# Gate and up of a routed feed-forward with the weights held in the array, and shared tiles without products of their own

## The chip, the cores and the metric

One core of a Trainium2 chip (trn2) runs the kernel. The time is device microseconds of one execution; three executions of the kernel before gave 442.81, 445.03 and 445.61 us.

## The reference

A transformer block in f32 over 1024 tokens of 256 values: attention with 16 heads, mixed with a linear attention, and behind it a feed-forward of 8 experts of which each token takes two.

```python
def _L0_ffn_ref(x, router_w, gate_w, up_w, down_w):
    B, S, H, F, E, K = (2, 128, 256, 688, 8, 2)
    b, s, h = x.shape
    xf = x.reshape(-1, h)
    logits = xf @ router_w.T
    top_v, top_i = jax.lax.top_k(logits, K)
    probs = jax.nn.softmax(top_v.astype(jnp.float32), axis=-1).astype(logits.dtype)
    combine = jnp.sum(jax.nn.one_hot(top_i, E, dtype=x.dtype) * probs[..., None], axis=1)
    g = jnp.einsum('th,efh->etf', xf, gate_w)
    u = jnp.einsum('th,efh->etf', xf, up_w)
    y = jnp.einsum('etf,ehf->eth', jax.nn.silu(g) * u, down_w)
    out = jnp.einsum('te,eth->th', combine, y)
    return out.reshape(b, s, h)
x = x + _L0_attn_ref(_layernorm(x, axis=-1), ...)
x = x + _L0_ffn_ref(_layernorm(x, axis=-1), ...)
```

## The kernel before, in words

The kernel is written for the five engines one by one, each with its own order of work and semaphores between them. The first 280 us are attention; the feed-forward's weights are fetched meanwhile (GpSimd, `load_gate_up`, one transfer for an expert), and the routing of the first half of the tokens is done in between. The expert part follows.

**Rows and tiles.** Each token's normalised row of 256 values, with its weight, its number and whether the expert is its first or second choice, is scattered by GpSimd into a list for its expert in memory (`scatter`, `xg_d`). The lists are worked off in tiles of 128 rows (`TILES`): tile A of an expert is rows 0 to 127 of its list, B rows 128 to 255, and a shared tile M takes rows 256 to 287 of four experts, 32 of each. The order is A of experts 0 to 4, M of experts 0 to 3 and of 4 to 7, B of experts 0 to 7, A of experts 5 to 7: 18 tiles. Rows beyond 288 of an expert would go through a loop behind it (`more`), which is skipped when there are none.

**One tile.** SyncE loads the rows (`load_xg`). TensorE turns them (`turn_x`, line 1480), VectorE copies them out of PSUM (`xgT_copy`, lines 1111 and 1107) and notes weights and token numbers (`take_meta`). TensorE multiplies with the turned rows held in the array and the expert's gate and up weights streamed, 4 chunks of 344 columns with two halves of H each (`columns`, `gate_up`; all matmuls pass the helper on line 1227). Gate is in PSUM banks 0 and 1, up in 2 and 3. ScalarE applies SiLU (line 792) and VectorE multiplies it with up (`hidden`, line 1115). The product has its 688 values along the free dimension; TensorE turns it in six blocks (`turn_hidden`, line 1491), VectorE copies it (`hidT_copy`, lines 1123 and 1124), and TensorE multiplies it with the down weights, six chunks of 256 columns (`down`, `products`). For a shared tile each of these calls is made four times, for strips of 32 rows. ScalarE weights the result (`tile_weigh`, line 796), and GpSimd adds its rows into memory with an indirect transfer (`add_y`, line 647): once for a tile, twice for a shared one (tokens of first and of second choice apart).

**The order.** From tile 3 on TensorE runs `gate_up(t)`, `turn_x(t + 1)`, `down(t - 1)`, `turn_hidden(t)`; the first three tiles are threaded by hand between the end of attention and the routing of the second half of the tokens (`post(1, ...)`). VectorE runs `take_meta(t)`, `xgT_copy(t + 1)`, `hidden(t)`, `hidT_copy(t)`. An addition waits for the landing of the one before it. The sum of the first 15 tiles (`DIRECT`) is made in `sum_d`; when these have landed, SyncE copies it to the output (line 504), and the last three tiles are added there. These are the lines in which GpSimd's order is set:

```python
if t:
    pool.wait_ge(y_added, 16 * adds(t - 1))
if t == DIRECT:
    pool.wait_ge(out_done, 16)
pool.wait_ge(y_ready, t + 1)
for k in range(K if shared(t) else 1):
    if k:
        pool.wait_ge(y_added, 16 * adds(t) - 16)
    add_rows(t, k, sum_d if t < DIRECT else out_v, y_added)
```

Of the kernel before, what the change touches and what calls it, by code (L numbers as in the profile page):

```python
# [14 lines left out]
P = 128  # L15
# [5 lines left out]
FB = [P, P, P, P, 88, 88]  # L21
FO = [sum(FB[:i]) for i in range(len(FB))]
FN = F // 2
# [3 lines left out]
UR = 32  # L27
# [53 lines left out]
def block_kernel(nc, x_d, w_d, rope_d, const_d, gate_d, router_d, gu_d, dn_d, out_d):  # L81
    ctx = ExitStack()
    with ctx:
# [50 lines left out]
        yt = words(A + 12288, NY + 1, H)  # L134
        tmp_odd = words(A + 14336, 4, HALF)
# [78 lines left out]
        xgT = keep(2, HB, P)  # L214
        act_g = keep(2, F)
        hid = keep(2, F)
        hidT = keep(2, len(FB), P)
# [8 lines left out]
        def sem(name):  # L226
# [34 lines left out]
        more_in, more_x_ps, more_x, more_gu, more_silu, more_hid, more_h_ps, more_h, more_y, more_yt, more_taken, more_added, more_done = (  # L261
            sem(n) for n in ("more_in", "more_x_ps", "more_x", "more_gu", "more_silu", "more_hid", "more_h_ps", "more_h",
# [7 lines left out]
        hidT_ps, hidT_ready, y_ps, y_ready, y_added = (sem(n) for n in  # L270
            ("hidT_ps", "hidT_ready", "y_ps", "y_ready", "y_added"))
# [95 lines left out]
        def loads(t):  # L367

            return sum(PER if shared(n) else 1 for n in range(t % 2, t + 1, 2))
# [5 lines left out]
        def needs(t):  # L375

            return E if any(E - 1 in experts(n) for n in range(t + 1)) else E - 1

        def place(i, t):

            return 2 * i + t // STEPS, t % STEPS, 2 * STEPS * i + t

# [4 lines left out]
        def _(sp):  # L387
# [91 lines left out]
            def load_xg(t):  # L479

                kind, e = TILES[t]
                if kind == "M":
                    for j in range(PER):
                        row = (PER * e + j) * T + 2 * P
                        sp.dma_start(xg[UR * j:UR * j + UR, t % 2], xg_d[row:row + UR, :]).then_inc(xg_in[t % 2], 16)
                else:
                    row = e * T + (P if kind == "B" else 0)
                    sp.dma_start(xg[:, t % 2], xg_d[row:row + P, :]).then_inc(xg_in[t % 2], 16)
# [7 lines left out]
            for t in range(2, NT):  # L496
                if t == 3:
                    start_sum(1)
                if t == E - ENDS:
                    sp.wait_ge(scattered[1], 16 * K * 4)  # L500
                sp.wait_ge(xgT_ready, t - 1)
                load_xg(t)
# [11 lines left out]
            with sp.If(some):  # L514
                sp.wait_ge(more_again, 16 * ENDS)
                with sp.Fori(0, NMORE) as i:
                    with sp.If_lt(sp.to_reg(i), more):
                        row = sp.value_load(row_i[0:1, bass.ts(i, 1)], min_val=0, max_val=E * T)
                        sp.dma_start(xg[:, 0], xg_d[bass.ds(row, P), :]).then_inc(more_in, 16)
                        sp.wait_ge(more_added, 16 * i + 16)  # L520
# [6 lines left out]
        def _(pool):  # L527
# [143 lines left out]
            pool.dma_start(gu[:, E - 1], gu_d[:, E - 1]).then_inc(gu_in, 16)  # L671
# [22 lines left out]
        def _(act):  # L694
# [96 lines left out]
            def silu(par):  # L791
                return nc.scalar.activation(act_g[:, par].rearrange("p (b c) -> p b c", b=2), psum[:, 0:2, 0:FN], ACT.Silu)  # L792

            def weigh(t):

                return nc.scalar.activation(yt[:, t % NY if t < NT else NY], psum[:, 6, 0:H], ACT.Copy, scale=weight_y[:, t:t + 1])  # L796

            def tile_silu(t):
                act.wait_ge(gu_ps, t + 1)
                silu(t % 2).then_inc(silu_ready, 1)  # L800
# [14 lines left out]
            for t in range(3, NT):  # L815
                tile_silu(t)
                tile_weigh(t - 1)
# [4 lines left out]
            with act.If(some):  # L822
                with act.Fori(0, NMORE) as i:
                    with act.If_lt(act.to_reg(i), more):
                        act.wait_ge(more_gu, i + 1)
                        silu(0).then_inc(more_silu, 1)
# [5 lines left out]
        def _(dve):  # L832
# [273 lines left out]
            def turned_x(par):  # L1106
                return V.tensor_copy(xgT[:, par], psum[:, 7, 0:HB * P].rearrange("p (b c) -> p b c", b=HB))

            def xgT_copy(t):
                dve.wait_ge(xgT_ps, t + 1)  # L1110
                V.tensor_copy(meta[:, t % 2], xg[:, t % 2, H:ROW])  # L1111
                turned_x(t % 2).then_inc(xgT_ready, 1)

            def times(par):
                return V.tensor_tensor(hid[:, par].rearrange("p (b c) -> p b c", b=2),  # L1115
                                       act_g[:, par].rearrange("p (b c) -> p b c", b=2), psum[:, 2:4, 0:FN], ALU.mult)

            def hidden(t):
                dve.wait_ge(silu_ready, t + 1)
                times(t % 2).then_inc(hid_ready, 1)  # L1120

            def turned_hidden(par):
                V.tensor_copy(hidT[:, par, 0:4], psum[:, 4].rearrange("p (c t) -> p c t", c=4))  # L1123
                return V.tensor_copy(hidT[0:FB[4], par, 4:6], psum[0:FB[4], 5, 0:2 * P].rearrange("p (c t) -> p c t", c=2))

            def hidT_copy(t):
                dve.wait_ge(hidT_ps, t + 1)
                turned_hidden(t % 2).then_inc(hidT_ready, 1)

            def take_meta(t):  # L1130

                dve.wait_ge(xgT_ready, t + 1)
                m = meta[:, t % 2]
# [30 lines left out]
            hidT_copy(0)  # L1164
# [10 lines left out]
            hidT_copy(1)  # L1175
# [421 lines left out]
```

## Time and profile before

| | us |
|---|---|
| median of three executions | 445.03 |
| lowest, highest | 442.81, 445.61 |
| the profiled execution, whole | 448.04 |
| the profiled execution, span from the first to the last instruction | 446.1 |
| TensorE busy in the span | 405.4 (91%) |
| VectorE, ScalarE, GpSimd busy | 267.7, 198.2, 98.2 |

The profile is of one execution. Times in it are microseconds from its first instruction. A row of the timeline is one or more instructions of a kind in succession: start, time from the first start to the last end, engine, line, operation, output<-input, shapes, count, and in brackets the idle time before it and what ended it. A matmul's end is modelled and includes its drain, so successive matmuls overlap, and a stretch of TensorE is better read from start to start. An f32 matmul leaves two records, a turn (transpose) one.

### The profile page before, as it was taken

How to read it: one execution, taken by the hardware profiler on the slowest of the kernel's cores; microseconds unless marked ns; L12 is line 12 of the kernel's file. 1: busy time of each engine (PE TensorE's matmuls, PEld its weight loads, DVE VectorE, ACT ScalarE, POOL GpSimd, SP SyncE). 2: the span in 40 equal slices, each digit the busy share in tenths (PEclk: the TensorE clock that was granted, in tenths of full speed). 3: DMA queues.
4: the chain of work that ended last, by engine and by line, in shares of the span. 5: the costliest groups of instructions: out<-in, count | busy, mean ns of one | idle time of the engine just before them, and what ended most of it. 6: DMA issues, size and time to landing. Idle time of an engine off the chain costs nothing.

```text
span 446.1 us, 6508 instructions
## 1 busy us (share of the span) xinstructions
PE 405.4 (91%) x2144; PEld 202.0 (45%) x2145; DVE 267.7 (60%) x513; ACT 198.2 (44%) x349; POOL 98.2 (22%) x92
## 2 busy tenths in 40 slices
PE   0887799979999999999999799999999999999992
PEld 0526175222222232342332123577665677777771
DVE  6498899866888888779979610278233233233230
ACT  0236825756676766657656598411111111111110
POOL 6100660421011011001014220006421421212112
PEclk9998589998999999999989999999999999999997
DMA  6227674467264453203013169525422232211131
GB/s 201 106 71 141 108 176 95 121 209 240 97 206 148 162 190 113 63 1 129 0 39 138 49 232 337 160 72 186 84 37 37 40 44 37 35 36 25 24 107 24
DMA packets 24409, 48.15 MB, mean 108 GB/s; under 512 B 4448, under 2 KB 17888, under 8 KB 22528
## 3 DMA queue, kind: packets, MB, share of 16 engines
q0 software_dynamic: 7824, 30.27, 22.7%
q1 hardware_dynamic: 15984, 15.96, 14.4%
q10 hardware_dynamic: 576, 1.58, 1.1%
q8 instruction: 16, 0.26, 0.3%
q14 instruction: 9, 0.07, 0.1%
HBM read 30.05 MB, written 18.74 MB: 109 GB/s over the span
## 4 chain that ended last, share of the span: by engine, by line
PE 72%; DVE 12%; DMA 5%; issue 2%; ACT 2%; SPq 2%; another core or an unknown queue 2%; POOL 1%; DVEq 0%; POOLq 0%; ACTq 0%
PE psum L1227 66%; DVE mem L948 6%; PE psum L1491 2%; DMA parts_d<-mem 2%; DMA mem<-x 1%; ACT mem L778 1%; DMA mem<-mem 1%; PE psum L1351 1%; PE psum L1480 1%; SPq L432 1%; DVE mem L1013 1%; DMA out<-mem 1%; DVE mem L885 1%; POOL mem L539 1%
## 5 line engine op out<-in xcount | busy, mean ns | idle before, releaser
L1227 PE MATMUL psum<-mem 128*32 128x512 f32 (+10 forms) x1904 | 381.3, 461 | 18.6 <-DMA mem<-parts_d 2.8
L1227 PEld LDWEIGHTS psum<-mem 128*32 128x32 f32 (+4 forms) x1904 | 173.0, 134 | 205.0 <-issue 84.1
L948 DVE TENSOR_REDUCE mem<-psum 128x1 f32<-128x1024 f32 x128 | 152.1, 1219 | 33.3 <-PE psum L1227 30.3
L778 ACT ACTIVATE mem<-psum 128x512 f32<-128x512 f32 x256 | 137.3, 604 | 64.8 <-PE psum L1227 59.5
L792 ACT ACTIVATE mem<-psum 128x688 f32<-128x688 f32 x18 | 13.4, 746 | 85.6 <-PE psum L1227 79.4
L647 POOL DMA_INDIRECT sum_d<-mem x17 | 26.6, 1564 | 79.4 <-ACT mem L796 63.4
L1111 DVE COPY mem<-mem 128x3 f32<-128x3 f32 x18 | 3.0, 169 | 57.6 <-PE psum L1480 52.5
L1123 DVE COPY mem<-psum 128x512 f32<-128x512 f32 x18 | 12.5, 692 | 28.4 <-PE psum L1491 27.5
L796 ACT ACTIVATE mem<-psum,mem 128x256 f32<-128x256 f32 x18 | 8.5, 474 | 40.8 <-PE psum L1227 36.6
L599 POOL DMA_DIRECT2D mem<-gate_up x7 | 4.0, 572 | 75.8 <-DMA mem<-mem 75.8
L1115 DVE TENSOR_TENSOR mem<-mem,psum 128x688 f32<-128x688 f32 x18 | 15.7, 870 | 5.0 <-ACT mem L792 4.3
L623 POOL DMA_INDIRECT xg_d<-mem x16 | 15.7, 979 | 6.1 <-issue 4.5
L978 DVE RECIPROCAL mem<-psum 128x16 f32<-128x16 f32 x8 | 2.1, 258 | 24.2 <-PE psum L1351 24.2
L1491 PE MATMUL psum<-mem 128*128 128x128 f32 (+1 forms) x108 | 14.9, 274 | 0.9 <-DVE mem L1115 0.9
L593 POOL DMA_DIRECT2D xg_d<-mem x9 | 8.0, 891 | 34.5 <-PE psum L1227 29.0
L1234 PE MATMUL psum<-mem 128*128 128x128 f32 x16 | 3.9, 425 | 12.5 <-DVE mem L852 12.5
L549 POOL COPY mem<-mem 128x512 f32<-128x512 f32 x8 | 4.8, 610 | 46.0 <-ACT mem L716 30.9
L1491 PEld LDWEIGHTS psum<-mem 128*128 128x128 f32 (+1 forms) x108 | 12.4, 135 | 3.7 <-DVE mem L1115 1.3
L539 POOL TENSOR_TENSOR mem<-mem 128x2 f32<-128x2 f32 (+1 forms) x6 | 5.2, 864 | 22.6 <-DVE mem L847 22.6
L708 ACT CAST mem<-mem 128x512 bf16<-128x512 f32 (+1 forms) x7 | 4.7, 677 | 10.8 <-DVE mem L891 10.8
L1234 PEld LDWEIGHTS psum<-mem 128*128 128x128 f32 x16 | 3.1, 223 | 12.5 <-issue 11.4
L885 DVE TENSOR_TENSOR mem<-psum,mem 128x512 f32<-128x512 f32 x8 | 5.5, 686 | 5.1 <-PE psum L1227 5.1
(121 smaller groups left out, 199.4 us busy)
## 6 DMA issues: line engine op xcount, KB each, us to landing
mem<-gate_up POOLq DMA_DIRECT2D x8, 1376.0 KB
xg_d<-mem POOLq DMA_DIRECT2D x8, 1036.0 KB, 5.9
mem<-down POOLq DMA_DIRECT2D x4, 1024.0 KB, 10.4
mem<-parts_d SPq DMA_DIRECT2D x24, 128.0 KB, 4.3
mem<-parts_d SPq DMA_DIRECT2D x48, 64.0 KB, 2.3
parts_d<-mem SPq DMA_DIRECT2D x18, 128.0 KB, 1.8
mem<-xg_d SPq DMA_DIRECT2D x16, 129.5 KB
mem<-down POOLq DMA_DIRECT2D x2, 704.0 KB, 12.6
```

Of the source, the lines that this page charges most:

```text
L539: nc.gpsimd.tensor_tensor(rstd[:, c], rstd[:, c], half_c[:, c], ALU.pow).then_inc(rstd_ready, 1)
L623: pool.indirect_dma_start(out=xg_d, out_offset=bass.IndirectOffsetOnAxis(ap=slot[:, hf, k, n:n + 1], axis=0), in_=xn2[:, n, k], in_offset= ...
L647: pool.indirect_dma_start(out=to, out_offset=bass.IndirectOffsetOnAxis(ap=token_y[:, t, k:k + 1], axis=0), in_=yt[:, t % NY if t < NT else ...
L778: nc.scalar.activation(prob[:, t % 8], psum[:, score_bank(n, t)], ACT.Exp, scale=HD ** -0.5).then_inc(exp_ready, 1)
L792: return nc.scalar.activation(act_g[:, par].rearrange("p (b c) -> p b c", b=2), psum[:, 0:2, 0:FN], ACT.Silu)
L796: return nc.scalar.activation(yt[:, t % NY if t < NT else NY], psum[:, 6, 0:H], ACT.Copy, scale=weight_y[:, t:t + 1])
L885: V.tensor_tensor(m[:, 2 * b], psum[:, p + b], rope[:, 0, c], ALU.mult)
L948: V.tensor_reduce(mx[:, par, k:k + 1], banks(2 * (k % 2), 2), AX.X, ALU.max).then_inc(max_ready, 1)
L1115: return V.tensor_tensor(hid[:, par].rearrange("p (b c) -> p b c", b=2), act_g[:, par].rearrange("p (b c) -> p b c", b=2), psum[:, 2:4, 0: ...
L1123: V.tensor_copy(hidT[:, par, 0:4], psum[:, 4].rearrange("p (c t) -> p c t", c=4))
L1227: return nc.tensor.matmul(*a, **k)
L1491: ins = nc.tensor.transpose(psum[0:n, 4 + c // 4, (c % 4) * P:(c % 4 + 1) * P], hid[:, par, o:o + n], ident)
```

## The change

Gate and up are computed the other way round: 128 columns of an expert's weights are held in the array and the rows are streamed, so the result has the 688 values along the partitions and needs no turn before the down product. F is cut into 128, 128, 128, 128, 112 and 64 (was 4 x 128 and 2 x 88). The weights of an expert lie as gate, the last 64 of up, the first 624 of up, so that the last 64 columns of gate and of up are one piece of 128. A tile's gate and up are 11 pieces of two calls (`columns`), in two halves: half 0 has gate in bank 0 and up in bank 1 (3 pieces each), half 1 gate in bank 2 (2 pieces and the joint one) and up in bank 3 (2 pieces). SiLU is three instructions, the product three, written into one of five buffers of hidden values (`hidT`).

A shared tile has no gate and up of its own. Its rows are loaded and turned early, before the first B tile of its experts, into a tile of their own (`xgT_m`, from bank 6), and 32 of them are copied behind the 128 rows of each B tile (`WIDE` = 160). Its down product takes columns 128 to 159 of the four B tiles' hidden values. The order is A0 to A4, B0 to B3, M0, B4 to B7, M1, A5 to A7. `GATED` are the 16 tiles with gate and up, `ROWS_IN` the order in which rows are loaded and turned. The result of down alternates between banks 4 and 5. Of the hand-threaded start, the turns of products and their waits go; one wait for the second half's slots goes, and one for the residual sum moves. The loop for rows beyond 288 fetches its expert's weights anew. GpSimd's additions are as before.

```diff
-FB = [P, P, P, P, 88, 88]
+FB = [P, P, P, P, 112, 64]
-TILES = ([("A", e) for e in range(E - ENDS)] + [("M", m) for m in range(E // PER)] + [("B", e) for e in range(E)]
+TILES = ([("A", e) for e in range(E - ENDS)]
+         + [t for m in range(E // PER) for t in [("B", PER * m + j) for j in range(PER)] + [("M", m)]]
          + [("A", e) for e in range(E - ENDS, E)])
+GATED = [t for t in range(NT) if TILES[t][0] != "M"]
+ROWS_IN = sorted(range(NT), key=lambda t: t - PER - 0.5 if TILES[t][0] == "M" else t)
+WIDE = P + UR
+NHID = 5
...
+        def rows_behind(g):
+
+            at = lambda n: ROWS_IN.index(GATED[n])
+            return range(at(g) + 1, at(g + 1) + 1)
...
+        def gate_up_pieces(to, src):
+
+            end = FO[5]
+            return [(to[:, :, 0:F], src[:, :, 0:F]), (to[:, :, F:F + FB[5]], src[:, :, F + end:]),
+                    (to[:, :, F + FB[5]:], src[:, :, F:F + end])]
...
-                pool.dma_start(gu[:, e], gu_d[:, e]).then_inc(gu_in, 16)
+                for to, src in gate_up_pieces(gu[:, e], gu_d[:, e]):
+                    pool.dma_start(to, src).then_inc(gu_in, 16)
...
+            def silu(half, n):
+
+                m = 3 - half
+                ins = nc.scalar.activation(act_g[:, half, 0:m, 0:n], psum[:, 2 * half, 0:m * n].rearrange("p (c t) -> p c t", c=m),
+                                           ACT.Silu)
+                if half:
+                    ins = nc.scalar.activation(act_end[0:FB[5], 0:n], psum[0:FB[5], 2, 2 * n:3 * n], ACT.Silu)
+                return ins
...
-            for t in range(3, NT):
-                tile_silu(t)
-                tile_weigh(t - 1)
+            for g in range(3, len(GATED)):
+                tile_silu(g)
+                for t in range(GATED[g - 1], GATED[g]):
+                    tile_weigh(t)
...
+            def xgT_copy(x):
+                t = ROWS_IN[x]
+                kind, e = TILES[t]
+                dve.wait_ge(xgT_ps, x + 1)
+                V.tensor_copy(meta[:, x % 2], xg[:, x % 2, H:ROW])
+                if kind == "M":
+                    V.tensor_copy(xgT_m, psum[:, 6, 0:HB * P].rearrange("p (b c) -> p b c", b=HB)).then_inc(xgT_ready, 1)
+                    return
+                par = GATED.index(t) % 2
+                if kind == "B":
+                    j = e % PER
+                    dve.wait_ge(xgT_ready, ROWS_IN.index(TILES.index(("M", e // PER))) + 1)
+                    V.tensor_copy(xgT[:, par, :, P:], xgT_m[:, :, UR * j:UR * j + UR])
+                turned_x(par).then_inc(xgT_ready, 1)
...
+            def hidden(g):
+                for half in range(2):
+                    dve.wait_ge(silu_ready, 2 * g + half + 1)
+                    if half == 0 and g >= NHID:
+                        dve.wait_ge(y_ps, last_use(g - NHID) + 1)
+                    times(half, g % NHID, wide(g)).then_inc(hid_ready, 1)
...
-            for t in range(3, NT):
-                take_meta(t)
-                if t + 1 < NT:
-                    xgT_copy(t + 1)
-                hidden(t)
-                hidT_copy(t)
+            take_meta(3)
+            for g in range(3, len(GATED)):
+                if g + 1 < len(GATED):
+                    for n in rows_behind(g):
+                        xgT_copy(n)
+                        take_meta(n)
+                hidden(g)
...
-                            ins = mm(psum[r, c, 0:FN], xgT[:, par, b, r], gu[:, e, b, c * FN:(c + 1) * FN],
-                                     start=(b == 0), stop=(b == HB - 1), skip_group_check=len(es) > 1)
+                        ins = mm(psum[0:m, 2 * half + up, k * n:(k + 1) * n], gu[:, e, b, c:c + m], xgT[:, par, b, 0:n],
+                                 start=(b == 0), stop=(b == HB - 1))
...
+                if g and 0 in ups:
+                    pe.wait_ge(hid_ready, 2 * g + half - 1)
...
-            for t in range(3, NT):
-                gate_up(t)
-                if t + 1 < NT:
-                    turn_x(t + 1)
-                down(t - 1)
-                turn_hidden(t)
+            for g in range(3, len(GATED)):
+                for half in range(2):
+                    gate_up(g, half)
+                if g + 1 < len(GATED):
+                    for n in rows_behind(g):
+                        turn_x(n)
+                for t in range(GATED[g - 1], GATED[g]):
+                    down(t)
             down(NT - 1)
```

## Rows read from the trace of the kernel before

**Rows 1.** The page, part 1: busy us (share of the span) xinstructions, by engine.

```profile
PE 405.4 (91%) x2144; PEld 202.0 (45%) x2145; DVE 267.7 (60%) x513; ACT 198.2 (44%) x349; POOL 98.2 (22%) x92
```

**Rows 2.** Windows: stretch, length, busy us and instructions per engine, granted clock, DMA.

```profile
320.00:438.00 118.00, 116.89 (x683) 83.60 (x682) 36.77 (x107) 17.08 (x28) 27.23 (x18) 1.00 0.25 43
```

**Rows 3.** Timeline of TensorE, a tile's period and the end: start, us, engine, line, form.

```profile
410.22 4.79 PE L1227 MATMUL psum<-mem 128*128 128x344 f32 x16
414.85 0.38 PE L1480 MATMUL psum<-mem 128*128 128x128 f32 x2
415.07 2.76 PE L1227 MATMUL psum<-mem 128*128 128x256 f32 x12
417.66 0.82 PE L1491 MATMUL psum<-mem 128*128 128x128 f32 x6
...
435.57 2.86 PE L1227 MATMUL psum<-mem 128*128 128x256 f32 x12 [1.11 <-DVE mem L1124]
```

**Rows 4.** Timeline of TensorE: a shared tile's gate and up, and its down.

```profile
328.19 4.83 PE L1227 MATMUL psum<-mem 128*32 128x344 f32 x64
...
341.71 2.80 PE L1227 MATMUL psum<-mem 128*32 128x256 f32 x48
```

**Rows 5.** Timeline of TensorE: loads of 128x128 with 136 and 8 columns; the form's mean.

```profile
71.22 0.86 PE L1227 MATMUL psum<-mem 128*128 128x136 f32 x6
...
L1227 PE MATMUL psum<-mem 128*128 128x136 f32 x64 | 9.1, 280 | 0.5 <-DVE mem L966 0.5
...
299.10 1.48 PE L1227 MATMUL psum<-mem 128*128 128x8 f32 x12
```

**Rows 6.** Timeline of VectorE and ScalarE in one tile's period.

```profile
415.05 0.75 ACT L792 ACTIVATE mem<-psum 128x688 f32<-128x688 f32 x1 [4.75 <-PE psum L1227]
...
415.35 0.42 DVE L1107 COPY mem<-psum 128x256 f32<-128x256 f32 x1
415.83 0.87 DVE L1115 TENSOR_TENSOR mem<-mem,psum 128x688 f32<-128x688 f32 x1
```

**Rows 7.** The chain that ended last, in order of time, at the expert part's start.

```profile
290.21 0.77 DVE mem L1115
...
294.16 1.39 DVE mem L1013 x4
...
296.69 0.29 PE psum L1227
```

**Rows 8.** Timeline of TensorE: tile 1, and around tile 3.

```profile
289.72 2.55 PE L1227 MATMUL psum<-mem 128*128 128x344 f32 x8 [0.16 <-ACT mem L792]
...
304.58 2.83 PE L1227 MATMUL psum<-mem 128*128 128x256 f32 x12 [0.36 <-issue]
...
308.07 7.46 PE L1227 MATMUL psum<-mem 128*128 128x256 f32 x28
...
319.29 0.88 PE L1491 MATMUL psum<-mem 128*128 128x128 f32 x6 [0.94 <-DVE mem L1115]
```

**Rows 9.** Timeline of GpSimd: additions of a shared tile, each behind a landing.

```profile
354.36 1.55 POOL L647 DMA_INDIRECT sum_d<-mem  x1 [2.96 <-DMA sum_d<-mem]
358.46 1.56 POOL L647 DMA_INDIRECT sum_d<-mem  x1 [2.54 <-DMA sum_d<-mem]
```

**Rows 10.** Timeline of GpSimd and SyncE at the end.

```profile
419.16 1.56 POOL L647 DMA_INDIRECT sum_d<-mem  x1 [6.54 <-ACT mem L796]
...
422.97 0.61 SPq L504 DMA_DIRECT2D out<-sum_d  x1
...
429.11 1.55 POOL L647 DMA_INDIRECT out<-mem  x1 [8.38 <-DMA out<-sum_d]
...
439.78 1.55 POOL L647 DMA_INDIRECT out<-mem  x1 [3.06 <-ACT mem L796]
```

**Rows 11.** Timeline: GpSimd's issue of four weight loads; SyncE's load of shared rows.

```profile
261.07 2.17 POOL L644 DMA_DIRECT2D mem<-down  x4
...
316.93 3.62 SPq L485 DMA_DIRECT2D mem<-xg_d  x8
```

More of the change, by code:

```diff
@@ L1118, in hidden @@
[L1118 to L1128, printed above, removed]
@@ new lines, in times @@
+            def times(half, slot, n):
+                m = 3 - half
+                ins = V.tensor_tensor(hidT(slot)[:, 3 * half:3 * half + m, 0:n], act_g[:, half, 0:m, 0:n],
+                                      psum[:, 2 * half + 1, 0:m * n].rearrange("p (c t) -> p c t", c=m), ALU.mult)
+                if half:
+                    ins = V.tensor_tensor(hidT(slot)[0:FB[5], 5, 0:n], act_end[0:FB[5], 0:n],
+                                          psum[FB[5]:, 2, 2 * n:3 * n], ALU.mult)
+                return ins
@@ L1454, in steps, with columns @@
                     turn_x(0)
-            def columns(par, es, chunks):
-                for c in chunks:
+            def columns(par, e, n, half, up):
+                pieces = [((F + FB[5] if up else 0) + FO[c], FB[c]) for c in ((0, 1, 2), (3, 4))[half]]
+                if half and not up:
+                    pieces.append((FO[5], 2 * FB[5]))
+                for k, (c, m) in enumerate(pieces):
                     for b in range(HB):
-                        for j, e in enumerate(es):
-                            r = slice(0, P) if len(es) == 1 else slice(UR * j, UR * j + UR)
-                            ins = mm(psum[r, c, 0:FN], xgT[:, par, b, r], gu[:, e, b, c * FN:(c + 1) * FN],
-                                     start=(b == 0), stop=(b == HB - 1), skip_group_check=len(es) > 1)
-                return ins
@@ new lines, in columns, with gate_up @@
+                return ins
+            def gate_up(g, half, ups=(0, 1)):
+                e = TILES[GATED[g]][1]
+                if half == 0 and 0 in ups:
+                    pe.wait_ge(xgT_ready, ROWS_IN.index(GATED[g]) + 1)
+                    pe.wait_ge(gu_in, 48 * needs(g))
+                if g and 0 in ups:
+                    pe.wait_ge(hid_ready, 2 * g + half - 1)
+                for up in ups:
+                    ins = columns(g % 2, e, wide(g), half, up)
+                if 1 in ups:
@@ L1501, in products, with turn_x @@
-            def products(par, es):
+            def turn_x(x):
+                pe.wait_ge(xg_in[x % 2], 16 * loads(x))
+                if x:
+                    pe.wait_ge(xgT_ready, x)
+                turned(x % 2, 6 if shared(ROWS_IN[x]) else 7).then_inc(xgT_ps, 1)
+            def products(to, slots, es, r):
                 for c, n in enumerate(FB):
                     for j, e in enumerate(es):
-                        r = slice(0, P) if len(es) == 1 else slice(UR * j, UR * j + UR)
-                        ins = mm(psum[r, 6, 0:H], hidT[0:n, par, c, r], dn[0:n, c, e], start=(c == 0),
+                        o = slice(0, P) if len(es) == 1 else slice(UR * j, UR * j + UR)
+                        ins = mm(psum[o, to, 0:H], hidT(slots[j])[0:n, c, r], dn[0:n, c, e], start=(c == 0),
@@ L1559, in _ @@
                         e = pe.value_load(ex_i[0:1, bass.ts(i, 1)], min_val=0, max_val=E - 1)
[L1560 to L1561 removed]
+                        pe.wait_ge(more_in, 64 * i + 64)
+                        turned(0, 7).then_inc(more_x_ps, 1)
                         pe.wait_ge(more_x, i + 1)
[L1563 removed]
+                        for half in range(2):
+                            for up in range(2):
+                                ins = columns(0, 0, P, half, up)
+                        ins.then_inc(more_gu, 1)
                         pe.wait_ge(more_hid, i + 1)
[L1565 to L1567 removed]
+                        products(4 + NT % 2, [0], (e,), slice(0, P)).then_inc(more_y, 1)
 def kernel(**inputs):
```

166 lines of the change are left out of this document (70 added, 96 removed).

## Prediction

> **What bounds the kernel now.** The page comes first: TensorE is busy for 91% of the span [rows 1]. Last I read what is behind TensorE's end, GpSimd's additions and SyncE's copy [rows 9, 10], because there the end is made: an addition into memory is waited for before the next is issued. Now that chain has slack; TensorE (its last group starts at 435.57 [rows 3] and takes 2.59) stands ahead of the last addition, and from its end at 438.16 to 446.10 there are 7.9 us.
>
> **What the change does to a period.** Gone: the turns of the products (0.66 a tile, 18 tiles), VectorE's copies of them, and the shared tiles' own gate and up (2 x 4.83). New: gate and up hold 128 columns of weights and stream the rows: 11 pieces x 2 halves of H = 22 calls, 44 records, of 128 columns for an A tile and 160 for a B tile; over 16 tiles 704 records. Price of one: the nearest row has just this form, a fresh f32 weight load of 128x128 for every record and 136 streamed columns: six records span 0.86 us, of which the last takes 0.28, so (0.86-0.28)/5 = 116 ns [rows 5], which is 136 x 0.833 + 2.5. With 8 columns, where the load alone counts, twelve span 1.48 us; with about the same 0.28 for the last (an estimate) that is 1.20/11 = 109 ns [rows 5]. So the load is hidden behind the columns already at 136. I take 109 ns for 128 columns (bounds: 107, the columns alone, and 116) and 136 ns for 160 (133 to 143). A: 44 x 109 = 4.80 us. B: 44 x 136 = 5.98. Periods: A 4.80+0.22+2.59 = 7.61, 0.49 less than now; B 5.98+0.22+2.59 = 8.79, 0.69 more; a shared tile keeps only its down, 2.73 by starts, and one more turn of rows.
>
> The Trainium skill speaks against such short groups: TensorE: Matmul & The Clock Gate, section Back-to-back issue gap, gives a stream of load and matmul pairs about 81 ns at 128 columns against 56 for the columns alone. By that each record would cost 25 ns more than its columns, 18 us in all, and the change would lose; the 136-column row, at 2.5 ns over its columns, disagrees with it for this kernel's f32 form.
>
> **The waits that move.** VectorE in a period: copy of the turned rows, two small copies, then the product of half 0; TensorE may begin the next half 0 only then (same banks). After the turn: 0.42 for the rows, an estimated 0.17 for the small copy, 0.25 for the rider's 64 columns, 0.3 for the meta data (estimates from it), 0.65 for 480 columns (0.87 for 688 [rows 6]): 1.8 us, under the 2.59 of down. Margin 0.8; what would exceed it costs 1 for 1 in each of 13 periods. ScalarE: three SiLUs, about 0.6+0.5+0.4 us (0.75 for 688 columns [rows 6]) and the weighting, in 7.6: free. The SiLU and product of half 1 have the 3 us of the next half 0 as cover. A slot of hidden values is reused after five tiles, when its shared tile is done; free.
>
> Where a shared tile's rows are turned, the next tile's rows are turned directly behind them and wait for VectorE's copy: from 414.85 (turn) to 415.77 (end of the copy at 415.35+0.42) [rows 3, 6] is 0.9 us, so 0.97 with the hand-over, instead of 0.22. Twice, after tiles A4 and B3. Bounds 0.22 and 1.5.
>
> **The start of the part.** TensorE must now wait for the product of tile 0 (half 0), not only its SiLU, before tile 1: VectorE is at it at 290.21 [rows 7], the smaller product takes 0.56, so about 290.9 instead of 289.7 [rows 8]. In VectorE's queue the product of tile 0 in three pieces (1.25 against 0.85) stands before the second residual sum, so normalisation ends 0.6 later. Tile 2's half 0 waits for the product of tile 1, which stands behind the second four normalisations (1.39 [rows 7]): 298.1 instead of 296.7 [rows 7], and the router's logits end at about 302.5 instead of 300.6 (299.10+1.48 [rows 5]). Against that 1.9 TensorE saves three turns of products (2.0) and a wait of 0.36 [rows 8]: tile 3's gate begins at 310.5 instead of 310.7 (a down and a gate stand as 28 records from 308.07 [rows 8]). The wait of 0.94 us at 319.29 [rows 8] is for ScalarE and VectorE, which both came late for a reason that no row names; I count half of it (bounds 0 and 0.94).
>
> The routing of the second half comes 1.9 late too, and GpSimd issues three loads of the last expert's weights where it issued one: 0.54 each by the row of four [rows 11], mostly before the slots are ready. So scatter begins about 1.9 late, and instead of 316.93 [rows 11] SyncE starts the shared rows at 318.8; four loads at 0.46 and some 2 us of flight bring them at 322.7. They are wanted at 318.6+4.8 = 323.4: just free; a delay of 1 us more would cost 0.3. The other weight loads, each in three pieces (two more issues of 0.54), lie in the attention part, behind nothing that TensorE waits for; bounds 0 and 0.3 us each for contention, eight times.
>
> **The sum.** Tile 3 begins at 310.5; with 7.61 and the 0.5: A4 at 318.6. A4: 7.61+0.97 = 8.58, 327.2. B0 to B2: 26.4, 353.6. B3: 9.76, 363.3. B4 with the first shared down: 8.79+2.73 = 11.5, 374.8. B5 to B7: 26.4, 401.2. A5 up to the down of B7: 7.61, 408.8. TensorE then needs 2.73+7.61+4.80+2.59+2.59 = 20.3 to its end at 429.1, 9.1 earlier than now.
>
> But now the last tile before the copy out is the shared one, with two additions, right behind B7. From the end of a down (417.66, by starts) to its addition (419.16) it is 1.5 us [rows 3, 10]; an addition that waits for the one before it follows 4.1 behind it [rows 9]; from an addition to the copy 3.8, from the copy to the first addition into the result 6.1, from the last addition to the end 6.3 [rows 10]. So: addition of B7 at 410.3, shared 414.4 and 418.5, copy 422.3, additions 428.4, 432.5, 436.6, end 442.9. TensorE's own end would allow 429.1+7.9 = 437.0; the chain of additions comes out 5.9 later and takes that much of the 9.1. Span 442.9 against 446.1, 3.2 less. The profiled execution took 448.04 us for that span, the median of the runs 445.03: forecast 445.03-3.2 = **441.8 us**.
>
> **Rivals.** (1) *The chain is hidden anyway*, because its links close up or the two additions of the shared tile overlap what I count in series: then TensorE sets the end, 437.0 by the span, 9.1 less, 436 us. For it: nothing in the rows; the seven links would have to lose 5.9 us. Chance 0.1. (2) *The loads of the weights aren't hidden*: in every one of the 704 records load and columns stand behind each other. At full price, 109+107 ns, 704 x 0.11 = 77 us, 519 us. It decides at little: 11 ns a record, 7.7 us, eats the 3.2 and makes 1% slower, 449.5 us; the case where they are partly hidden stands at about 452. Against it: 116 ns at 136 columns, and 128 weight columns of f32 in both. Chance 0.08. The figure of the Trainium skill's page above, TensorE: Matmul & The Clock Gate, would give 441.8+18 = 460. (3) *VectorE is late for the next half 0*: 1 us beyond the margin in 13 periods gives 13 us, 455; the margin of 0.8 must be used up first. Chance 0.04. (4) *The chain is right but the front gains more or less*: the forecast's own spread: 0.5 (the stall), 2 x 0.7 (the turns), 704 x 3 ns = 2, chain links +-0.2 x 7 = 1.4, contention up to 2.4. That is 441.8 -3 and +3.5, so 438.8 to 445.3. Chance of the forecast 0.78.
>
> **How the numbers follow.** A measurement of this kernel can tell about 1%, 4.5 us, from no change: faster is below 440.6. From the forecast's spread about a third lies there (0.26 of 0.78), and rival 1 (0.1): 0.36. Slower than 449.5: rivals 2 and 3 at most of their chance: 0.10. The rest, 0.54, within 1%. The range leaves out the far ends of rivals 2 and 3: 435.5 to 446.5.
>
> **What would show it.** Right: 44 records in 4.8 us (A) and 6.0 (B); periods of 7.6 and 8.8; TensorE's end near 429 and a gap of some 14 us behind it, in which GpSimd waits for additions to land; three additions in a row about 4.1 apart before the copy. Wrong: records of 160 columns more than 140 ns apart; TensorE waiting for VectorE at each half 0; the last addition started by ScalarE's weighting rather than by the landing before it; TensorE waiting near 323 for the shared rows; scores in the attention part held up while weights load.

## The result and the profile after

The change makes the kernel a little slower: 448.36 us against 444.59, medians of seven runs each, 3.8 us; the ratio, of the means, is 1.0093 (95% interval 1.007 to 1.0117). Two later comparisons, e5 and f2 on chips 5 and 15, gave 2.9 us and 1.006 (1.0043 to 1.0077), and 3.4 us and 1.0068 (1.0045 to 1.0091). The forecast was 441.8 us, 3.2 less than before, with 446.5 as its upper end.

The profiled execution of the changed kernel took 448.53 us, its span is 446.6. The page, part 1, against [rows 1]:

```profile
PE 400.8 (90%) x2356; PEld 223.6 (50%) x2357; DVE 256.5 (57%) x515; ACT 202.4 (45%) x379; POOL 110.9 (25%) x108
```

TensorE is busy for 4.6 us less, and VectorE for 11 us less. The timeline of TensorE in the expert part (start, us, engine, line, form, count; line 1289 is the helper for all matmuls, 1543 the turn of rows), against [rows 3, 4]; the two small rows at 322.62 and 323.79 are the turns of the shared tile's rows and of the first B tile's:

```profile
289.30 2.92 PE L1289 MATMUL psum<-mem 128*128 128x128 f32 x24 [1.25 <-DVE mem L1180]
...
296.37 7.18 PE L1289 MATMUL psum<-mem 128*128 128x128 f32 x68 [0.75 <-DVE mem L1180]
...
322.62 0.38 PE L1543 MATMUL psum<-mem 128*128 128x128 f32 x2
323.79 0.41 PE L1543 MATMUL psum<-mem 128*128 128x128 f32 x2 [0.79 <-DVE mem L1169]
...
333.03 0.38 PE L1543 MATMUL psum<-mem 128*128 128x128 f32 x2
333.24 9.15 PE L1289 MATMUL psum<-mem 128*128 128x256 f32 x56
342.23 0.38 PE L1543 MATMUL psum<-mem 128*128 128x128 f32 x2
...
401.74 8.04 PE L1289 MATMUL psum<-mem 128*128 128x256 f32 x56
409.62 0.38 PE L1543 MATMUL psum<-mem 128*128 128x128 f32 x2
```

A row of 56 records is a down (12) and the next tile's gate and up (44). By starts it takes 8.99 us where the tile is 160 wide and 7.88 where it is 128; the period is 9.20 and 8.10 with the turn. The forecast had 8.79 and 7.61. So an A tile costs what it cost before, 8.10, and a B tile 1.1 more. From tile 3 on TensorE waits twice, for 0.79 us at each of the two shared tiles' turns; ahead of that it waits for the products of tiles 1 and 2 (1.25 and 0.75).

The end, timeline of GpSimd (additions, line 690) and SyncE's copy, against [rows 9, 10]:

```profile
414.12 1.56 POOL L690 DMA_INDIRECT sum_d<-mem  x1 [6.54 <-ACT mem L846]
418.17 1.56 POOL L690 DMA_INDIRECT sum_d<-mem  x1 [2.49 <-DMA sum_d<-mem]
422.23 1.56 POOL L690 DMA_INDIRECT sum_d<-mem  x1 [2.50 <-DMA sum_d<-mem]
...
426.01 0.61 SPq L542 DMA_DIRECT2D out<-sum_d  x1
...
432.18 1.56 POOL L690 DMA_INDIRECT out<-mem  x1 [8.39 <-DMA out<-sum_d]
436.22 1.56 POOL L690 DMA_INDIRECT out<-mem  x1 [2.49 <-DMA out<-mem]
440.21 1.56 POOL L690 DMA_INDIRECT out<-mem  x1 [2.43 <-DMA out<-mem]
```

The addition of B7 is released by ScalarE; every later one by the landing of the one before or by the copy: this is the chain of additions. TensorE's last record ends at 434.6, and 12.0 us follow instead of 7.7 (both read with the last record's drain). From the addition of B7 to the end it is 32.5 us, and the forecast had 32.6.

### The profile page after: what moved, and what is told of

It is laid out like the page before. It is cut to its first block, busy times and chain, and to the rows that moved or that the text cites. A ratio compares the mean times of both kernels' runs of the same rounds, so it can differ in the third digit from the quotient of the medians.

```text
span 446.6 us, 6970 instructions
## 1 busy us (share of the span) xinstructions
PE 400.8 (90%) x2356; PEld 223.6 (50%) x2357; DVE 256.5 (57%) x515; ACT 202.4 (45%) x379; POOL 110.9 (25%) x108
## 4 chain that ended last, share of the span: by engine, by line
PE 67%; DVE 14%; DMA 9%; issue 4%; SPq 2%; ACT 1%; POOL 1%; DVEq 0%; POOLq 0%; ACTq 0%
PE psum L1289 64%; DVE mem L1002 7%; DMA sum_d<-mem 3%; DMA parts_d<-mem 2%; DMA mem<-x 1%; DMA mem<-mem 1%; DMA out<-sum_d 1%; DVE mem L1067 1%; ACT mem L822 1%; PE psum L1413 1%; PE psum L1543 1%; SPq L470 1%; DVE mem L939 1%; PE psum L1326 1%; POOL out L690 1%
## 5 line engine op out<-in xcount | busy, mean ns | idle before, releaser
L1289 PE MATMUL psum<-mem 128*32 128x512 f32 (+15 forms) x2224 | 386.7, 406 | 18.6 <-DVE mem L940 3.8
L1289 PEld LDWEIGHTS psum<-mem 128*128 128x128 f32 (+8 forms) x2224 | 207.4, 145 | 185.9 <-issue 88.5
L838 ACT ACTIVATE mem<-psum 128x384 f32<-128x384 f32 (+3 forms) x32 | 15.0, 471 | 73.7 <-PE psum L1289 73.7
L642 POOL DMA_DIRECT2D mem<-gate_up x21 | 15.1, 722 | 74.1 <-DMA mem<-mem 73.9
L1180 DVE TENSOR_TENSOR mem<-mem,psum 128x384 f32<-128x384 f32 (+3 forms) x32 | 15.5, 522 | 5.7 <-ACT mem L838 4.0
L1296 PE MATMUL psum<-mem 128*128 128x128 f32 x16 | 3.9, 426 | 12.7 <-DVE mem L906 12.7
L1296 PEld LDWEIGHTS psum<-mem 128*128 128x128 f32 x16 | 3.1, 223 | 12.7 <-issue 11.6
L672 POOL TENSOR_TENSOR mem<-mem 128x4 f32<-128x4 f32 x2 | 2.0, 1013 | 27.3 <-DVE mem L1078 27.3
L1543 PE MATMUL psum<-mem 128*128 128x128 f32 x36 | 7.0, 275 | 1.6 <-DVE mem L1169 1.6
L690 POOL DMA_INDIRECT out<-mem x3 | 4.7, 1557 | 13.3 <-DMA out<-sum_d 8.4
```

Of the source, the lines that this page charges most:

```text
L642: pool.dma_start(to, src).then_inc(gu_in, 16)
L690: pool.indirect_dma_start(out=to, out_offset=bass.IndirectOffsetOnAxis(ap=token_y[:, t, k:k + 1], axis=0), in_=yt[:, t % NY if t < NT else ...
L838: ins = nc.scalar.activation(act_g[:, half, 0:m, 0:n], psum[:, 2 * half, 0:m * n].rearrange("p (c t) -> p c t", c=m), ACT.Silu)
L1180: ins = V.tensor_tensor(hidT(slot)[:, 3 * half:3 * half + m, 0:n], act_g[:, half, 0:m, 0:n], psum[:, 2 * half + 1, 0:m * n].rearrange("p ( ...
L1289: return nc.tensor.matmul(*a, **k)
L1543: ins = nc.tensor.transpose(psum[:, to, b * P:(b + 1) * P], xg[:, par, b * P:(b + 1) * P], ident)
```

## Experiments

**The kernel before, profiled again.** It is unchanged, on two chips.

> The kernel before once more, unchanged, for a second profile. Theory: the profiled execution from which the forecast was made was not a typical one; it held waits of 2.3 us (ScalarE, attention part) and of about 2 us (ScalarE and VectorE near 317 us) for which no row names a cause, and its 448.04 us lie 3 us over the median. A second profile then has neither wait and a span near 443. Rival: the waits belong to the kernel; they stand at the same places again, the span is 446 again, and the 3 us are what profiling costs.

> The kernel before, unchanged, for a profile on the same chip as the changed kernel. Two profiles of it so far have ScalarE and VectorE waiting for about 2 us near 250 and near 317 us without a named cause, and the stretch between the seventh and the eighth mixing of attention (245 to 266 us) takes 21 us in both; all five profiles of the changed kernel that fetch weights in three pieces have neither and take 18.9. Theory: this differs by chip, not by kernel: where the runs of the kernel before are near 444.6, its profile shows a span of 442.7, 18.9 us and no such wait. Rival: it belongs to the kernel; 21 us again.

| kernel before | runs on that chip | span | mixing 7 to mixing 8 | TensorE's wait near 317 |
|---|---|---|---|---|
| profile of the forecast | 445.03 (442.81 to 445.61), chip not on record | 446.1 | 21.2 | 0.94 |
| e1, chip 6 | 447.78 (446.09 to 449.98) | 446.3 | 20.7 | 1.03 |
| f1, chip 15 | 444.42 (443.49 to 447.06) | 442.5 | 18.9 | none |

The rows are VectorE's reciprocals at the head of two mixings of attention's output (timeline), and TensorE and ScalarE near tile 3. In e1:

```profile
245.37 0.26 DVE L978 RECIPROCAL mem<-psum 128x16 f32<-128x16 f32 x1 [0.94 <-PE psum L1351]
...
266.06 0.26 DVE L978 RECIPROCAL mem<-psum 128x16 f32<-128x16 f32 x1 [9.96 <-PE psum L1351]
...
317.52 0.74 ACT L792 ACTIVATE mem<-psum 128x688 f32<-128x688 f32 x1 [6.26 <-remote]
...
319.23 0.88 PE L1491 MATMUL psum<-mem 128*128 128x128 f32 x6 [1.03 <-DVE mem L1115]
```

In f1:

```profile
244.66 0.26 DVE L978 RECIPROCAL mem<-psum 128x16 f32<-128x16 f32 x1 [0.36 <-PE psum L1351]
...
263.60 0.26 DVE L978 RECIPROCAL mem<-psum 128x16 f32<-128x16 f32 x1 [9.97 <-PE psum L1351]
...
312.96 0.74 ACT L792 ACTIVATE mem<-psum 128x688 f32<-128x688 f32 x1 [4.15 <-PE psum L1227]
```

So neither rival of e1 was right as it stood: the waits came back there, and profiling does not cost 3 us (e1 and f1 lie at their chips' medians). f1 came out as expected: on a chip whose runs are near 444.4 the waits are absent. All four profiles with the long stretch (the forecast's, e1, e2, e4) have both waits, and none of the nine others has either. The three that have a chip on record are of chip 6; the nine are of chips 5 and 15 and the changed kernel's first profile. The profile that the forecast read looks like chip 6, and the runs shown with it like the others; that it came from such a chip is inferred. Why the engines stand just behind the two groups of scatters (which end at 249 and at 315) stays open.

**The cut of F alone, in the kernel before.**

```diff
-FB = [P, P, P, P, 88, 88]
+FB = [P, P, P, P, 112, 64]
```

> The kernel before with only the cut of F changed, 128 x 4, 112, 64 for 128 x 4, 88, 88; nothing else. Theory: a down product over 64 partitions costs four exposed weight loads a tile, 0.39 us (records 306 to 320 ns apart where 216 are due), whatever the rest of the kernel is; 18 tiles give +7.0 us, ratio 1.016, and the records show the same 306 and 320. Rival: the gaps belong to the new kernel (its 160 wide buffers, its bank change); then the records stay 216 apart and the ratio is 1.000.

Measured 452.57 us against 447.78, 4.8 us by the medians, ratio 1.0101 (1.0072 to 1.0131), below the 1.016 that was expected. The timeline of TensorE shows down now at 2.89 us by starts where it was 2.59 [rows 3]. The turns behind it take 0.80 ahead of a shared tile, where the kernel before has 0.75 at the same place (327.44 to 328.19), and 0.72 elsewhere, where it has 0.66:

```profile
325.28 2.95 PE L1227 MATMUL psum<-mem 128*128 128x256 f32 x12
328.17 0.87 PE L1491 MATMUL psum<-mem 128*128 128x128 f32 x6
328.97 4.83 PE L1227 MATMUL psum<-mem 128*32 128x344 f32 x64
...
421.75 0.88 PE L1491 MATMUL psum<-mem 128*128 128x128 f32 x6
422.47 4.79 PE L1227 MATMUL psum<-mem 128*128 128x344 f32 x16
```

The rival falls: the gaps need nothing of the new kernel, only the new cut (of its two sizes, the next run tells which). The single records are 307, 321 and 306 ns apart, as expected, and the next one 165 where 114 were: 0.35 us a tile, 0.30 in down and 0.05 behind it, not 0.39. Sixteen tiles of that are 5.6; the two shared tiles' downs, in strips, lose 0.14 each (2.87 for 2.73 by starts), 5.9 in all. Against e1 on the same chip, 0.9 less is lost in the wait near tile 3, which leaves 5.0: the difference of the two spans (451.3 and 446.3), and near the 4.8 of the medians.

**96 partitions in the last chunk.** `DB` is the cut of the down product; the weights' rows 64 to 95 of that chunk are zeros from the host.

```diff
+DB = FB[:5] + [96]
...
             reciprocal_root(slice(4, 8), 6)
+            pool.wait_ge(rstd_ready, 6)
+            pool.memset(hidT_first[FB[5]:DB[5], :, 5], 0.0).then_inc(zero_set, 1)
+            pool.wait_ge(zero_set, 1)
+            pool.memset(hidT_more[FB[5]:DB[5], :, 5], 0.0).then_inc(zero_set, 1)
+            pool.wait_ge(zero_set, 2)
...
-                for c, n in enumerate(FB):
+                for c, n in enumerate(DB):
```

An earlier form of it (e3), without waits between GpSimd's clears, gave no time. The changed kernel was run beside it:

> The changed kernel once more, so that its variants are compared on one chip. Theory: ratio to the kernel before 1.009. Its expert part, from the last turn of attention's output to the end, is 164.3 us again (162.4 in the kernel before); what differs from execution to execution lies ahead of it or in one wait near tile 3.

> The changed kernel with the last chunk of the down product over 96 partitions instead of 64: rows 64 to 95 are zeros in the weights (from the host's layout) and in the hidden values (two memsets of GpSimd while it is idle). Theory: the exposed loads of weights go, 0.39 us in each tile, 0.29 of it in down and 0.1 at the next gate; TensorE's end and the chain of additions come 6 us earlier: ratio 0.9955. Rival: 112 partitions break the rhythm, or the number of partitions does not matter: ratio 1.009.

e5: 447.47 us, ratio 1.006 where 1.009 was expected. e6: 444.02 against 444.56, ratio 0.9988 (0.997 to 1.0006), 3.5 us less than e5 where 6 were expected, and no difference to the kernel before that is clear of noise. The timeline of TensorE in e6, one B tile and an A tile:

```profile
313.10 7.65 PE L1295 MATMUL psum<-mem 128*128 128x256 f32 x56
320.59 0.38 PE L1549 MATMUL psum<-mem 128*128 128x128 f32 x2
...
330.82 8.76 PE L1295 MATMUL psum<-mem 128*128 128x256 f32 x56
339.42 0.38 PE L1549 MATMUL psum<-mem 128*128 128x128 f32 x2
```

8.60 instead of 8.99 and 7.49 instead of 7.88: the 0.39 us of a tile are gone, with more rows in the array, not fewer. The 112 stayed, so it is the 64. With down at 2.59 the 44 records of gate and up take 6.01 and 4.90, 137 and 111 ns each; the forecast had 136 and 109.

The loads of weights (engine PEld) show how. In the changed kernel the load for the first record over 64 partitions, and again the first one over 128 behind them, starts only together with its own matmul, after an idle 0.33 us; in e6 seven loads around the same place follow without such a gap, each at the start of the matmul before its own. After, then e6:

```profile
335.50 0.29 PEld L1289 LDWEIGHTS psum<-mem 64*128 64x128 f32 x2 [0.33 <-issue]
336.12 0.43 PEld L1289 LDWEIGHTS psum<-mem 128*128 128x128 f32 x3 [0.33 <-issue]
...
332.34 1.41 PEld L1295 LDWEIGHTS psum<-mem 112*128 112x128 f32 x7
```

Why did 0.39 a tile bring only 3.5? The executions reach the last mixing of attention at different times (VectorE's reciprocal at 282.77 in the changed kernel's first profile, at 281.53 in e6), so I count from there. TensorE's last record then ends 5.5 us earlier (146.3 for 151.8), and the addition of B7, with which the chain begins, starts 4.4 earlier (126.9 for 131.3): only twelve tiles' downs lie ahead of it, and 0.4 are given back at the start. There GpSimd's clears run beside VectorE's eight normalisations, which take 3.06 us instead of 2.67, and TensorE waits for them. So GpSimd was idle, but the clears were not free. After, then e6:

```profile
293.09 2.67 DVE L1067 TENSOR_SCALAR mem<-mem 128x256 f32<-128x256 f32 x8
...
291.84 3.06 DVE L1073 TENSOR_SCALAR mem<-mem 128x256 f32<-128x256 f32 x8
```

The rest is in the chain itself. Timeline of GpSimd, e6:

```profile
408.45 1.56 POOL L691 DMA_INDIRECT sum_d<-mem  x1 [6.15 <-ACT mem L852]
414.12 1.56 POOL L691 DMA_INDIRECT sum_d<-mem  x1 [4.11 <-DMA sum_d<-mem]
418.08 1.56 POOL L691 DMA_INDIRECT sum_d<-mem  x1 [2.40 <-DMA sum_d<-mem]
```

The first link takes 5.67 instead of 4.05. The DMA view of the stretch 408.4 to 414 has, beside the addition's packets, one of instructions, and the addition lands after 5.4 us instead of 3.8:

```profile
q8 instruction: 1, 0.02, 1.8%
issues: line engine op xcount, KB each, median us to landing
sum_d<-mem POOLq DMA_INDIRECT x1, 5.4
```

That packet is a fetch of instructions, 16 KB. It starts at 411.22 and takes 1.61 us. When the other packets of the addition are done, at 411.81, six are left, and they start one behind the other from 412.81 on, when the fetch ends. The DMA view of 412.80 to 413.45 has these six alone:

```profile
q0 software_dynamic: 6, 0.01, 9.7%
```

The changed kernel's first profile has such a packet beside the addition of 414.12 too, from 417.38 on for 0.98 us; no packet of the addition waits for its end (the last one starts at 417.54), and the link stays 4.05. In eight profiles (the changed kernel's and those of its variants on chips 5 and 15) twelve links are over 5.1 us (5.15 to 5.89), and in all twelve the addition's last packets start within 0.02 us of the end of a fetch; where an addition follows the one before directly, no other link is over 4.71. So a fetch that comes before an addition's last packets holds them up; on which DMA engine a packet runs is not in the trace. In e6 that is the whole 1.6 us; in e7 and f4 a third of the 1.7 lies behind the last packet and stays open. It also explains two profiles that lie beyond their runs: e8's, 443.81 against a median of 440.31, has two such links in its last chain (5.60 and 5.63), and in e5 the chain's first link takes 5.15, which makes its stretch from the last mixing to the end 164.8 us where the changed kernel's first profile has 163.8; the expectation was the same length again.

**The chain of additions.** Two variants of e6. In e7 the copy comes once, behind all additions (`DIRECT = NT`, and the wait for the redone additions in the skipped loop goes); in e8 the last shared tile has one addition instead of two.

```diff
-DIRECT = NT - ENDS
+DIRECT = NT
```

```diff
-                for k in range(K if shared(t) else 1):
+                for k in range(K if shared(t) and t < DIRECT - 1 else 1):
```

> As e6, and the copy to the output comes once, behind all 18 tiles' additions, instead of before the last three. Theory: the chain of additions sets the end. Six additions at 4.05 us from the down of B7, then the copy: 1.5+5x4.05+3.8+5.4+0.5 = 31.5 us against 34; with the last tile's product at 22.1 the last addition is just no longer late. 2 us less than e6: ratio 0.991. Rival: the end belongs to TensorE; then the copy stands behind its last product and the kernel is 4 us longer than e6: ratio 1.005.

> As e6, without the second addition of the last shared tile (the rows of four experts that are their tokens' second choice aren't added, so a part of the result is missing). Theory: one link of the chain goes and TensorE has 5.9 us behind it to spare, so the whole 4.05 us shows: ratio 0.9865. Rival: the additions are hidden behind TensorE; nothing changes against e6.

e7: 442.70, ratio 0.9956 (0.994 to 0.9973), 1.3 us less than e6 where 2 were expected. e8: 440.31, ratio 0.9891 (0.9867 to 0.9914), 3.7 less than e6 where 4.05 were expected. Both have the sign of the chain and neither that of TensorE as the end. The ratios that were expected, 0.991 and 0.9865, lie outside the intervals because e6, from which they were counted, had missed its own. In e7 the six additions follow each other without TensorE (the row at 418.07 names ScalarE, but it comes 4.10 behind the one before, like the others), and the copy starts at 434.11, 6.6 us behind TensorE's last record:

```profile
408.15 1.56 POOL L690 DMA_INDIRECT sum_d<-mem  x1 [6.15 <-ACT mem L851]
413.97 1.56 POOL L690 DMA_INDIRECT sum_d<-mem  x1 [4.25 <-DMA sum_d<-mem]
418.07 1.56 POOL L690 DMA_INDIRECT sum_d<-mem  x1 [2.55 <-ACT mem L851]
422.09 1.56 POOL L690 DMA_INDIRECT sum_d<-mem  x1 [2.46 <-DMA sum_d<-mem]
426.28 1.56 POOL L690 DMA_INDIRECT sum_d<-mem  x1 [2.63 <-DMA sum_d<-mem]
430.25 1.56 POOL L690 DMA_INDIRECT sum_d<-mem  x1 [2.41 <-DMA sum_d<-mem]
```

**One transfer for an expert's weights.** The host lays gate and up out in the core's order; the three transfers become one.

```diff
-                for to, src in gate_up_pieces(gu[:, e], gu_d[:, e]):
-                    pool.dma_start(to, src).then_inc(gu_in, 16)
+                pool.dma_start(gu[:, e], gu_d[:, e]).then_inc(gu_in, 16)
...
-    gate_up = np.concatenate([f["ffn_gate_w"], f["ffn_up_w"]], 1)
+    gate_up = np.concatenate([f["ffn_gate_w"], f["ffn_up_w"][:, FO[5]:], f["ffn_up_w"][:, 0:FO[5]]], 1)
```

> The changed kernel with an expert's gate and up weights laid out by the host in the order in which the core wants them, so that one transfer of 11008 bytes a partition fetches them instead of three. Theory: the three pieces cost nothing that TensorE sees; 448.4 us, within 1 us, ratio to the kernel before 1.008. Rival: part of the miss is the weight loads' contention and GpSimd's 1.5 us for each in the attention part: 2 to 4 us less, ratio 1.002.

> The changed kernel beside f1 on one chip. Theory: ratio 1.007; span 2.7 to 3.8 us over f1's on a chip of the quick kind, the difference all behind 283 us: tiles 0.39 us longer each than forecast, and the chain of additions. On a chip of the slow kind both are some 3 us longer.

> The changed kernel with one transfer for an expert's gate and up weights, now beside the changed kernel on the same chip. Theory: the three pieces cost nothing; within 0.2% of f2. Rival: the one transfer is the slower way by 2 us (it was 1.0137 times the kernel before on another chip, where f2's kernel was not run), or the quicker one.

e4 gave 453.67, ratio 1.0137 (1.01 to 1.0174), on chip 6 and without the changed kernel beside it: nothing follows for the transfers, as TensorE waits 1.79 us near tile 3 there. f3 beside f2 decides: 448.26 us against 447.79, 1.0071 (1.0047 to 1.0094) against 1.0068. The three pieces cost nothing that these runs can tell.

f2's span is 446.5, 4.0 over f1's, a little more than the 2.7 to 3.8 expected. Of that 3.2 lie behind the last mixing and 0.4 between the last two mixings (18.33 us instead of 17.97), where more of tile 0's gate and up is done: 24 records of 128 columns instead of 8 of 344. All nine profiles of the changed kernel and its variants have these 0.4.

**All of it, and two waits shorter.** e7 with these edits:

```diff
                 if x:
-                    pe.wait_ge(xgT_ready, x)
+                    pe.wait_ge(xgT_ready, x - 1 if shared(ROWS_IN[x - 1]) else x)
...
+            hidden(1)
             for n in range(4):
                 second_norm(1, 1, n)
-            hidden(1)
```

> As the variant with 96 partitions and the copy at the end, and two waits shorter: the rows of the first B tile are turned without waiting for VectorE's copy of the shared tile's rows (another bank), and VectorE makes the product of tile 1 before the second four normalisations. Theory: TensorE gains 2 x 0.8 less 0.3 for VectorE's late half 0, and 0.75 at tile 2; the chain of additions begins about 2 us earlier, ratio 0.991 to the kernel before. Rival: VectorE is late for half 0 by what is gained; ratio 0.9956 as before.

440.24 us against 444.42, ratio 0.9884 (0.9849 to 0.9919): faster than both kernels. TensorE's timeline has the four turns (two of the shared tile's, two of the next) back to back, and no wait at tile 2:

```profile
295.10 7.11 PE L1294 MATMUL psum<-mem 128*128 128x128 f32 x68
...
320.11 0.60 PE L1548 MATMUL psum<-mem 128*128 128x128 f32 x4
320.55 8.90 PE L1294 MATMUL psum<-mem 128*128 128x256 f32 x56
```

The down and gate behind the turns take 0.14 and 0.24 more than the 8.60 of other B tiles; VectorE has the copies for two tiles ahead of its product there, which fits its being late by that. From the last mixing to the end it is 156.7 us, 2.4 less than e7, where the gain of 2 was expected; the two waits were not taken out one by one.

## Why the forecast was wrong, point by point

The step that failed is a term of the sum: the down product at 2.59 us in each tile's period. It measured 2.89, with 0.1 more at the record behind it. A reference time that held waits of its own, and a smaller term left out, add to the miss. The mechanism of the end was right.

**The change of a tile, mis-sized in down.** The step read "A 7.61, B 8.79" with down at 2.59 as before. It took over the price of the down product although the change alters its cut: the last chunk has 64 partitions instead of 88. The diff shows that in its first line. e2 shows that the new cut alone costs time in the kernel before, and e6 takes the cost away: 0.39 us a tile. Gate and up were right to 1 or 2%, so rival 2 (load and columns one behind the other) is false. A record of 160 columns takes 137 ns where 136 were forecast, one of 128 columns 111.6 where 109 were, and there the load sets the pace: the records of 8 columns [rows 5] are 111.5 ns apart. The forecast read them as 109, with an estimate of 0.28 us for the last record; that one takes 0.256.

The Trainium skill (TensorE: Matmul & The Clock Gate, section Back-to-back issue gap) gives about 81 ns for a load and matmul pair at 128 columns, against 56 for the columns alone. This f32 stream disagrees with the 25 between them: 4 to 5 ns over the 107 of its columns.

From the last turn of attention's output to the down of B7 the forecast had 125.1 us; it took 130.5 (282.3 to 412.8). The 5.4 are, to 0.2: eleven tiles' periods and one shared down, 4.9 (an A tile 0.49, a B tile 0.41); two downs ahead of tile 3, 0.6; the shared tiles' turns at 1.17 instead of 0.97, 0.4; and the half of the unexplained wait, which did not come, -0.5.

**The shared tile.** Right: it keeps only its down (2.86 for 2.73). The wait of the next rows' turn came where it was placed, twice.

**VectorE and half 0.** Right in the steady part: no wait of TensorE for a product from tile 3 on, so rival 3 is false. At the start the waits for the products of tiles 1 and 2 came, as 1.25 and 0.75; f4 shows the second to be avoidable.

**The end.** Right: the additions take over behind B7, one behind the other at 4.05, with copy and end as in the forecast (32.5 us for 32.6); e8 and e7 show it on the clock. Rival 1 is false. That the sum comes out to 0.1 owes something to luck: a link is 1.1 to 1.8 us longer when an instruction fetch falls before its last packets, as in e5 and e6, and this profile was spared.

**The kernel before as the measure.** The forecast set its sum against the span of 446.1, of a profiled execution 3 us over the median of the runs, and took the difference from the median. It did not ask what in the profile made the 3 us. From the last mixing to the end that profile has 162.0 us and f1, without the two waits, 160.9: 1.0 is not there on the quicker chips. The forecast had noticed only the wait near tile 3, and took half of it off the changed kernel.

**A term that was missing.** More of tile 0's gate and up now lies ahead of the last mixing: 0.4, which the forecast, counting from the last turn, left out.

Together: -3.2 forecast, +5.4 for the tiles and turns, -0.3 for the chain, +1.0 for the measure, +0.4 ahead of the last mixing: +3.3. The medians of the three comparisons differ by 3.8, 2.9 and 3.4.

Stage by stage, in us of the profiles (the kernel before is f1's; TensorE's end with its drain):

| | to the last mixing | from there to TensorE's end | behind it | span |
|---|---|---|---|---|
| kernel before, f1 | 281.6 | 153.1 | 7.8 | 442.5 |
| changed, first profile | 282.8 | 151.8 | 12.0 | 446.6 |
| 96 partitions, e6 | 281.5 | 146.3 | 14.5 | 442.3 |
| and one copy at the end, e7 | 281.2 | 146.3 | 12.7 | 440.3 |
| and two waits shorter, f4 | 282.0 | 143.7 | 12.9 | 438.7 |

Of the 9.1 us that the forecast gave TensorE, the changed kernel has 1.3. e6 shows that 6.8 were to be had with the same order of work; but with the chain behind it e6 as a whole is no faster than the kernel before.

**The range** ended at 446.5 because it held unknown costs of what the change adds, and nothing for what it alters in an operation that stays.

## What to carry to other kernels

A cut of a dimension is an edit of every operation that uses it: price them all anew. In a stream of f32 records over 112 and 128 partitions, a few over 64 cost 0.39 us, and zeros up to 96 took that away; sizes between 64 and 88 were not tried. Before taking columns off the bound engine, add up what is serial behind it; here the forecast's own sum had a chain of transfers, 4 us a link, take 5.9 of 9.1 us, and the runs bore the chain out. And where the profiled execution lies beyond the other runs, look for the waits in it that nothing explains, and leave them out on both sides. A transfer that others wait for can be 1.6 us late because of an instruction fetch: compare several profiles before a single link is read as a price.

## What the runs showed of the hardware

- f32 records over 64 partitions between others over 112 and 128: the last record over 112, both over 64 and the first behind them each took some 0.1 us more than their columns, 0.39 us for the group. Over 88, 96 and 112 partitions no such cost (2.59 for twelve of 256 columns [rows 3], and again in e6). The loads of weights stand bare there: the first one over 64 and the first one over 128 behind it start with their own matmul (335.50 and 336.12), where the others start at the matmul before. The same happens in the kernel before where strips of 32 columns follow turns: 201 ns from the last turn to the first strip, where turns are 109 apart. What makes the load wait is not shown.
- Loads of 128x128 f32 weights for every 128 streamed columns leave 111.6 ns a record, 107 being the columns; with 8 columns it is 111.5, so the load sets the pace there. At 160 columns it is 137, of which 133 are the columns.
- An instruction fetch of 16 KB takes 0.9 to 1.9 us. Where it comes before the last packets of an indirect addition, these start when it ends, and the link takes 5.15 to 5.89 us instead of 3.9 to 4.7 (twelve cases in eight profiles).
- Eight normalisations of VectorE took 3.06 us beside GpSimd's clears and 2.67 without them (e6 against the changed kernel).
- Chips differ: on chip 6 ScalarE and VectorE stand for 1 to 2 us behind each of the two groups of scatters, and its runs are 0.8% longer than chip 15's (447.78 against 444.42 for one kernel). One chip of three shows it, and its cause is open.
